# A decoder kernel: the order of projections and value products in a state-space layer, and of key products in the attention behind it

## The chip, the cores and the metric

The kernel runs on one core of a Trainium2 chip. It is one program for the whole two-layer decoder. The metric is the device time of one execution in microseconds (us); shown are the median and the extremes of three runs, and one further execution was taken by the hardware profiler. The engines are PE (TensorE, matmul), DVE (VectorE), ACT (ScalarE), POOL (GpSimd) and SP (SyncE, which here only issues DMAs). A product of one engine reaches another through SBUF or PSUM and a semaphore; each engine works its own list of instructions in order.

## The reference, cut to what matters

64 sequences of 128 tokens, width 128, go through two layers. The change touches two stages: the state-space layer L1_attn and the preparation of the values of the cross attention L1_xattn, and that cross attention.

```python
# state-space layer, E = 256 channels, N = 16 states
z = x @ W_in + b_in
xc, xr = z[..., :E], silu(z[..., E:])
xc = silu(conv(xc) + conv_b)                    # four taps
proj = xc @ x_proj_w                            # dt (16), B (16), C (16)
delta = softplus(dt @ dt_proj_w + dt_bias)      # the step size
h = exp(delta * A) * h + (delta * u) * B        # for each of 16 states, along time
y = sum_over_states(h * C) + u * D_param
out = (y * xr) @ W_out + b_out
# cross attention, 16 heads over a context of 77 tokens
q = x @ Wq + bq;  k = ctx @ Wk + bk;  v = ctx @ Wv + bv
out = softmax(q k^T / 8) v @ Wo + bo + x        # then layernorm
```

## The kernel before

**State-space layer** (`phase_scan`, L1522 on). The 64 sequences are worked in NG = 16 groups of four, so a tile is 128 partitions (channels) by 2 halves by 512 columns (4 x 128 tokens). Each group runs through 16 states, and each engine has a function `body(g, s)` with a loop `for n in range(states)`, into which all other work is hung by tests such as `if n == 5`. That hand-written place is what sets the order.

For a state n: ACT makes the decay factors, an exponential for each half (`decay_state`, L2030), into PSUM. POOL makes the drive (`drive_state`, L1877), three buffers deep. DVE scans both halves (`scan_state`, L2242) and, for the 13 inline states, multiplies by C (`read_state`, L2255); PE adds the result into `y_ps` by a product with the identity (`sum_state`, L2394). In the states 3, 7 and 13, called aside, POOL multiplies by C instead and PE adds three states later (`sum_aside`, L2402). ACT can write a half's decay only when DVE has scanned that half of the state before, as there is one PSUM buffer.

Between them stands work for the coming groups. PE: `turn` (transposes x of group g + 2), `project_bc` (dt, B and C for g + 1), `project_dt` (the step size product for g + 1), `project_conv` (two times four taps for g + 2), `project_res` (g + 2), and `project_out` for group g - 1. All use the two PSUM banks of `f_ps`. ACT copies these out: `copy_xT`, `copy_proj`, `take_raw` (the step size: an absolute value and a Relu), then `soft_exp` and `soft_ln` (with a table load before and one after), after which POOL's `make_delta` adds the two parts of the softplus. DVE gates y (`gate_y`) and adds the output to x (`leave_group`).

**Lots.** The same phase also multiplies the context by the attention's folded value and output weights and writes the result to DRAM: 39 lots of 128 context rows times 4 parts of 512 columns make 156 units. A unit is one matmul in a bank of `f_ps` (`make_lot`, L2322), one copy on ACT (`take_lot`, L2071) into one of three stage tiles, and one DMA on SP (`store_units`). The table `places` gives ten a group, each as (state in which PE makes it, bank, state in which ACT copies it; 16 and 17 are states 0 and 1 of the next group). So groups 0 to 14 have ten, group 15 has six.

SP's list in this phase holds, for each group, the loads of B and C rows (`load_b`, `load_c`), the store of these rows and the stores of the units, in a fixed order; a store waits for ACT's copy and whatever is behind it on SP waits too.

**Cross attention** (`phase_cross1`, L2518 on). It works one sequence a step, i from -7 to 65. In step i PE makes the scores of i + 2, turns the softmax of i (`turn_p`, three parts), multiplies it by the values (`mix`, the output), and makes the "front" work: four key products for seven elements ahead, until they run out, and one transpose of x for four ahead. The front products go in turn into the two banks of `f_ps` (`follow`: a product waits until the one two places before it has been copied by ACT). `plan[i]` splits the five into early, middle and late, and both PE and ACT take them in this order: PE early behind the second part of the turns, middle ahead of `mix`, late behind it; ACT early behind `copy_p(i, 1)`, middle ahead of the exponential of i + 2 (`exp`), late behind it. SP loads the values of element i + 2 (`load_values`); the first of these loads waits until all 156 units are in DRAM.

## Time and profile before

| | us |
|---|---|
| median of three runs | 2921.3 |
| lowest, highest | 2917.96, 2922.2 |
| profiled execution | 2918.92 |
| its span in the trace | 2917.0 |
| busy: PE, DVE | 2483.3, 2258.2 |
| busy: POOL, ACT | 2039.5, 1712.4 |

The span runs from the first to the last instruction in the trace; the device time of that same execution is 1.9 us longer. The scans of the state-space layer run from 1115 to 2073 us in the span, the scores of the attention from 2102 to 2637 us; these two stages are some half of the time. PE, DVE and POOL are all busy for most of the layer, so a share of busy time does not tell which one holds the others; the waits before single instructions in one group do.

### The profile page before, as it was taken

Reading aid. Unit: us, or ns where it says so; the run is one execution under the profiler, and the core shown is the slowest. Engines: PE = TensorE matmul, PEld = TensorE weight load, DVE = VectorE, ACT = ScalarE, POOL = GpSimd, SP = SyncE. Lnnn points to the kernel's source line nnn. Section 1 sums busy time; section 2 is a strip of 40 time slices with the busy share of each in tenths; the row PEclk is TensorE's granted clock in tenths of the full one; section 3 lists DMA queues with packets and bytes.
Section 4 is the critical chain, followed back from the end, with each engine's and each line's share of the span. In section 5 each row is a group of like instructions: output and inputs, shape, how many; then the busy total and the mean of one; then the engine's idle time right before and its main releaser. Section 6 shows DMA issues by size and latency. Waiting matters only on the chain. (4 is left out here: it accounts for less than half of the span.)

```text
span 2917.0 us, 43507 instructions
## 1 busy us (share of the span) xinstructions
PE 2483.3 (85%) x13043; PEld 1466.9 (50%) x13058; DVE 2258.2 (77%) x3693; ACT 1712.4 (59%) x3383; POOL 2039.5 (70%) x1817
## 2 busy tenths in 40 slices
PE   6969999899799957889999899897799999995555
PEld 4646666566556632333333333342367777773222
DVE  5979999666534469999899988999577777776887
ACT  7847777643222246767776676765355555554665
POOL 5539999567656638989999899998355555554454
PEclk9969999899899988999999999999999999997555
DMA  5911111011155535545545455555222222220000
GB/s 177 422 33 23 23 23 23 3 38 44 38 156 161 154 114 201 196 161 205 195 173 199 169 199 187 182 190 175 65 68 81 79 81 81 77 79 18 18 18 22
DMA packets 238424, 331.81 MB, mean 114 GB/s; under 512 B 46434, under 2 KB 186999, under 8 KB 217347
## 3 DMA queue, kind: packets, MB, share of 16 engines
q1 hardware_dynamic: 227538, 311.48, 32.5%
q0 software_dynamic: 9088, 16.94, 1.6%
q8 instruction: 105, 1.72, 0.2%
q14 instruction: 109, 0.89, 0.1%
q10 hardware_dynamic: 1584, 0.79, 0.1%
HBM read 231.45 MB, written 99.50 MB: 113 GB/s over the span
## 5 line engine op out<-in xcount | busy, mean ns | idle before, releaser
L1877 POOL TENSOR_TENSOR s_drive<-s_du,s_b_sb 128x1024 f32<-128x1024 f32 x256 | 599.8, 2359 | 30.9 <-DVE s_state_ps L2242 30.7
L2242 DVE TENSOR_TENSOR_SCAN s_state_ps<-s_decay_ps,s_drive 128x512 f32<-128x512 f32 x416 | 487.5, 1217 | 74.1 <-ACT s_decay_ps L2030 63.8
L2394 PE MATMUL s_y_ps<-s_read,w_ident 128*128 128x512 f32 x832 | 404.0, 612 | 73.9 <-DVE s_read L2255 73.4
L2030 ACT ACTIVATE s_decay_ps<-s_delta,neg_rate 128x508 f32<-128x508 f32 x512 | 342.4, 683 | 162.9 <-DVE s_state_ps L2242 151.5
L2394 PEld LDWEIGHTS s_y_ps<-s_read,w_ident 128*128 128x128 f32 x832 | 152.2, 192 | 306.7 <-issue 155.6
L2255 DVE TENSOR_TENSOR s_read<-s_state_ps,s_c_sb 128x1024 f32<-128x1024 f32 x208 | 254.6, 1224 | 7.2
L1421 POOL DMA_INDIRECT m_y_scratch<-e_y,e_index x156 | 152.5, 978 | 93.8 <-DVE e_y L1467 51.9
L2322 PE MATMUL s_f_ps<-w_c_wvo,s_lotT 128*128 128x512 f32 (+1 forms) x312 | 157.7, 603 | 45.5 <-ACT s_dtT L1998 20.8
L2684 POOL TENSOR_TENSOR c_share<-c_p,c_norm 128x1232 f32<-128x1232 f32 x64 | 147.5, 2305 | 65.3 <-DVE c_norm L2816 65.3
L2731 ACT ACTIVATE c_k<-c_f_ps,key_bias 128x308 f32<-128x308 f32 x256 | 132.4, 518 | 100.0 <-PE c_f_ps L2884 99.7
L742 ACT ACTIVATE b_pT<-b_turn_ps 77x512 f32<-77x512 f32 x256 | 144.3, 591 | 74.4 <-PE b_turn_ps L871 74.4
L2925 PE MATMUL c_turn_ps<-c_vp,c_pT 128*128 128x128 f32 (+1 forms) x1280 | 158.0, 279 | 21.3 <-ACT c_pT L2756 21.3
L2884 PE MATMUL c_f_ps<-c_ctxT,w_c_wqk 128*128 128x308 f32 x512 | 166.3, 430 | 7.1 <-DMA c_ctxT<-in_ctxT_dram 5.2
L2925 PEld LDWEIGHTS c_turn_ps<-c_vp,c_pT 128*128 128x128 f32 (+1 forms) x1280 | 147.7, 191 | 49.0 <-issue 49.0
L1045 POOL DMA_INDIRECT m_rows_scratch<-m_xs,m_index x128 | 128.2, 1002 | 60.4 <-issue 39.9
L676 POOL TENSOR_TENSOR b_p<-b_p,b_top 128x1232 f32<-128x1232 f32 x64 | 143.9, 2248 | 36.0 <-DVE b_top L803 36.0
L2797 DVE TENSOR_REDUCE c_top<-c_s_ps 128x16 f32<-128x1232 f32 x64 | 92.2, 1441 | 95.4 <-PE c_s_ps L2900 95.4
L2751 ACT ACTIVATE c_pT<-c_turn_ps 128x512 f32<-128x512 f32 x128 | 69.7, 595 | 150.4 <-PE c_turn_ps L2916 150.4
L2071 ACT ACTIVATE s_stage<-s_f_ps 128x512 f32<-128x512 f32 (+1 forms) x156 | 90.6, 590 | 106.1 <-PE s_f_ps L2322 104.7
L871 PE MATMUL b_turn_ps<-w_ident,b_p 128*77 128x128 f32 x1024 | 152.6, 282 | 0.0
L2900 PE MATMUL c_s_ps<-c_k,c_xT 128*128 128x308 f32 x512 | 148.5, 432 | 0.0
L2660 POOL TENSOR_TENSOR x<-c_xs,w_c_bo 128x128 f32<-128x128 f32 x64 | 31.2, 488 | 165.7 <-DVE c_xs L2792 165.7
(389 smaller groups left out, 6293.7 us busy)
## 6 DMA issues: line engine op xcount, KB each, us to landing
s_b_sb<-s_bc_scratch SPq DMA_DIRECT2D x64, 1024.0 KB, 5.8
s_c_sb<-s_bc_scratch SPq DMA_DIRECT2D x64, 1024.0 KB, 5.6
c_vp_scratch<-s_stage SPq DMA_DIRECT2D x152, 256.0 KB, 2.9
c_vp<-c_vp_scratch SPq DMA_DIRECT2D x64, 576.0 KB, 4.1
m_rows_scratch<-fill SPq DMA_DIRECT2D x33, 1040.0 KB, 27.1
e_w<-in_m_we_dram SPq DMA_DIRECT2D x39, 384.0 KB, 3.2
e_xg<-m_rows_scratch SPq DMA_DIRECT2D x39, 260.0 KB, 3.4
s_read<-m_y_scratch SPq DMA_DIRECT2D x32, 256.0 KB, 3.1
```

Of the source, the lines that this page charges most:

```text
L871: last = nc.tensor.transpose(turn_ps[0:S2, j % 2, r * 128:(r + 1) * 128], p[:, s, per * r + j, :], core.ident[:, :])
L1421: nc.gpsimd.indirect_dma_start(y_dram[:, :], bass.IndirectOffsetOnAxis(index[:, t % y_slots, j:j + 1], 0), y[:, t % y_slots, j, :], None, ...
L1877: nc.gpsimd.tensor_tensor(drive[:, (g * states + n) % drives, :, :], du[:, s, :, :], b_sb[:, n, :].unsqueeze(1).broadcast_to([128, halves, ...
L2030: nc.scalar.activation(decay[:, m, :, 1:], delta[:, s, m, :].rearrange("p (b t) -> p b t", t=T)[:, :, 1:], ACT.Exp, scale=core.neg_rate[:, ...
L2242: nc.vector.tensor_tensor_scan(home[:, h, :], decay[:, h, :, :].rearrange("p b t -> p (b t)"), drive[:, (g * states + n) % drives, h, :], ...
L2255: nc.vector.tensor_tensor(read[:, r % deep, :, :], state[:, :, :], c_sb[:, n // per_chunk % 2, n % per_chunk, :].unsqueeze(1).broadcast_to ...
L2322: nc.tensor.matmul(f_ps[0:lot_width(j), bank, :], lotT[:, j % lot_slots, 0:lot_width(j)], wvo[:, 4 * n:4 * n + 4, :].rearrange("p h d -> p ...
L2394: last = nc.tensor.matmul(y_ps[:, m, :], core.ident[:, :], read[:, r % deep, m, :], start=False, stop=False)
L2684: nc.gpsimd.tensor_tensor(share[:, i % 2, :].rearrange("p (s h) -> p h s", h=heads), p[:, i % p_slots, :, :], norm[:, i % 2, :].unsqueeze( ...
L2884: nc.tensor.matmul(f_ps[:, mine % 2, 0:GB * S2], core.w["c_wqk"][:, h, :], ctxT[:, g % 2, :], start=True, stop=True).then_inc(front_ready. ...
L2900: last = nc.tensor.matmul(scores[:, r, :, :], xT[:, i % xT_slots, :], k[:, g % 2, per * r:per * (r + 1), S2 * e:S2 * (e + 1)], start=True, ...
L2925: last = nc.tensor.matmul(y_ps, pT[0:width(c), i % 2, c, :], vp[0:width(c), i % vp_slots, c, :], start=(c == 0), stop=(c == lumps - 1))
```

## The change

It changes no arithmetic. In the layer's per-state lists:

- `project_dt` on PE goes from state 5 to 4, `take_raw` on ACT from 7 to 6, `soft_ln` from 9 to 10, POOL's `make_delta` from 11 to 12; `soft_exp` stays in 8. DVE's `leave_group` goes from state 4 to 3.
- The table of units becomes `slots_of(g)`: eight in each of groups 0 to 13, eighteen in group 14 (both banks in each of states 7 to 15), twenty-six in group 15 (bank 0 in states 0 to 13, bank 1 in 4 to 15). The places (3, 0, 5) and (7, 1, 9) are gone, and the second unit of state 6 is copied in state 9 instead of 8. 14 x 8 + 18 + 26 = 156.
- PE makes a state's units ahead of the projections of that state instead of behind them.
- SP's stores are placed by the state of the copy, and units left at the end are copied and stored behind the last group.

In the attention the order of the five front products becomes key, key, key, x, key, with the second and third in the middle part (before: the second alone). A load of values waits for the stores that its own element reads instead of all.

```diff
-        places = ((1, 0, 3), (3, 0, 5), (6, 0, 8), (6, 1, 8), (7, 1, 9), (10, 0, 12), (13, 0, 15), (13, 1, 15),
-                  (14, 1, 16), (15, 1, 17))
+        def slots_of(g):
+            if g < NG - 2:
+                return [(1, 0, 3), (6, 0, 8), (6, 1, 9), (10, 0, 12), (13, 0, 15), (13, 1, 15), (14, 1, 16), (15, 1, 17)]
+            if g == NG - 2:
+                return [(n, bank, n + 2) for n in range(7, states) for bank in range(2)]
+            return [(n, bank, n + 2) for n in range(states) for bank in range(2) if (n <= 13, n >= 4)[bank]]
...
-                    if n == 11 and ahead(g, 1):
+                    if n == 12 and ahead(g, 1):
                         make_delta(g + 1, 1 - s)
...
-                    if n == 7 and ahead(g, 1):
+                    if n == 6 and ahead(g, 1):
                         take_raw(g + 1, 1 - s)
                     if n == 8 and ahead(g, 1):
                         soft_exp(g + 1, 1 - s)
-                    if n == 9 and ahead(g, 1):
+                    if n == 10 and ahead(g, 1):
                         soft_ln(g + 1, 1 - s)
...
+            for unit in taken_at(NG, 0, states):
+                take_lot(unit)
...
-                    if n == 4 and behind(g, 1):
+                    if n == 3 and behind(g, 1):
                         leave_group(g - 1, 1 - s)
...
+                    for unit in made_at(g, n):
+                        make_lot(g, unit)
                     if n == 1 and behind(g, 1):
                         project_out(g - 1, 1 - s)
                     if n == 2 and ahead(g, 1):
                         project_bc(g + 1, 1 - s)
-                    if n == 5 and ahead(g, 1):
+                    if n == 4 and ahead(g, 1):
                         project_dt(g + 1, 1 - s)
...
-                    for unit in units_at("made", g, n):
-                        make_lot(g, unit)
...
             if on(i + ahead_turn):
-                here.append(("x", i + ahead_turn))
+                here.insert(len(here[:3]), ("x", i + ahead_turn))
...
-            plan[i] = (here[:1], here[1:2], here[2:])
+            plan[i] = (here[:1], here[1:3], here[3:])
...
-                if i == 0:
-                    for n, out in enumerate(lot_out):
-                        sp.wait_ge(out.sem, out.at(-(-(units - n) // len(lot_out)), 0))
+                stored = min(units, (((i + 1) * S2 - 1) // 128 + 1) * heads * 128 // 512)
+                for n, out in enumerate(lot_out):
+                    sp.wait_ge(out.sem, out.at(-(-(stored - n) // len(lot_out)), 0))
```

ACT in a middle group, from the decays of states 6 and 7 on, before. `s_decay_ps` are the decays (two a state), `s_stage` the copies of units, `s_conv_sig<-s_f_ps` and `s_delta` the two of `take_raw`, the other `s_conv_sig` the exponential and Ln of the softplus:

```order
L2030 ACTIVATE s_decay_ps<-s_delta,neg_rate 128x4x127 x4
L2008 ACTIVATE s_conv_sig<-s_f_ps 128x1024
L2009 ACTIVATE s_delta<-s_f_ps 128x1024
L2030 ACTIVATE s_decay_ps<-s_delta,neg_rate 128x4x127 x2
L2071 ACTIVATE s_stage<-s_f_ps 128x512 x2
L2013 ACTIVATE s_conv_sig<-s_conv_sig 128x1024
L2030 ACTIVATE s_decay_ps<-s_delta,neg_rate 128x4x127 x2
L2071 ACTIVATE s_stage<-s_f_ps 128x512
L2017 ACT_TABLE_LOAD
L2017 ACTIVATE s_conv_sig<-s_conv_sig 128x1024
L2030 ACT_TABLE_LOAD
L2030 ACTIVATE s_decay_ps<-s_delta,neg_rate 128x4x127 x4
```

And after, from `take_raw` on (line numbers being those of the changed kernel):

```order
L2006 ACTIVATE s_conv_sig<-s_f_ps 128x1024
L2007 ACTIVATE s_delta<-s_f_ps 128x1024
L2028 ACTIVATE s_decay_ps<-s_delta,neg_rate 128x4x127 x4
L2069 ACTIVATE s_stage<-s_f_ps 128x512
L2011 ACTIVATE s_conv_sig<-s_conv_sig 128x1024
L2028 ACTIVATE s_decay_ps<-s_delta,neg_rate 128x4x127 x2
L2069 ACTIVATE s_stage<-s_f_ps 128x512
L2028 ACTIVATE s_decay_ps<-s_delta,neg_rate 128x4x127 x2
L2015 ACT_TABLE_LOAD
L2015 ACTIVATE s_conv_sig<-s_conv_sig 128x1024
L2028 ACT_TABLE_LOAD
L2028 ACTIVATE s_decay_ps<-s_delta,neg_rate 128x4x127 x2
```

`take_raw` stands ahead of the decays of state 7 instead of behind them, one copy of a unit stands in state 8 instead of two, and Ln with its two table loads stands behind the decays of state 10.

PE in the same group, from the output product of the group before to the units of state 6, before. `s_f_ps<-w_c_wvo` are the units, `s_f_ps<-s_dtT` the step size product, `s_y_ps<-s_read` the sums (two matmuls a state):

```order
L2417 MATMUL s_f_ps<-w_s_w_out,s_res_gate 128x128 x8
L2322 MATMUL s_f_ps<-w_c_wvo,s_lotT 128x512
L2394 MATMUL s_y_ps<-s_read,w_ident 128x512 x2
L2363 MATMUL s_f_ps<-s_u,w_s_x_proj 48x512 x2
L2322 MATMUL s_f_ps<-w_c_wvo,s_lotT 128x512
L2394 MATMUL s_y_ps<-s_read,w_ident 128x512 x4
L2375 MATMUL s_f_ps<-s_dtT,w_s_dt_proj 128x512 x2
L2394 MATMUL s_y_ps<-s_read,w_ident 128x512 x2
L2402 MATMUL s_y_ps<-s_state_aside,w_ident 128x512 x2
L2322 MATMUL s_f_ps<-w_c_wvo,s_lotT 128x512 x3
```

And after, from the sums of states 0 and 1:

```order
L2390 MATMUL s_y_ps<-s_read,w_ident 128x512 x4
L2317 MATMUL s_f_ps<-w_c_wvo,s_lotT 128x512
L2413 MATMUL s_f_ps<-w_s_w_out,s_res_gate 128x128 x8
L2390 MATMUL s_y_ps<-s_read,w_ident 128x512 x2
L2358 MATMUL s_f_ps<-s_u,w_s_x_proj 48x512 x2
L2390 MATMUL s_y_ps<-s_read,w_ident 128x512 x2
L2371 MATMUL s_f_ps<-s_dtT,w_s_dt_proj 128x512 x2
L2390 MATMUL s_y_ps<-s_read,w_ident 128x512 x4
L2398 MATMUL s_y_ps<-s_state_aside,w_ident 128x512 x2
L2317 MATMUL s_f_ps<-w_c_wvo,s_lotT 128x512 x2
```

The unit of state 1 stands ahead of the output product, the one of state 3 is gone, and the step size product stands behind the sum of state 4 instead of 5.

PE in a middle step of the attention, from a step's scores (`c_s_ps`) to the next ones, before. `c_f_ps<-c_ctxT` are keys, `c_f_ps<-w_ident` the turn of x, `c_turn_ps<-c_vp` is mix:

```order
L2900 MATMUL c_s_ps<-c_k,c_xT 128x308 x4
L2916 MATMUL c_turn_ps<-w_ident,c_share 128x128 x8
L2884 MATMUL c_f_ps<-c_ctxT,w_c_wqk 128x308
L2916 MATMUL c_turn_ps<-w_ident,c_share 128x128
L2916 MATMUL c_turn_ps<-w_ident,c_share 80x128
L2884 MATMUL c_f_ps<-c_ctxT,w_c_wqk 128x308
L2925 MATMUL c_turn_ps<-c_vp,c_pT 128x128 x10
L2884 MATMUL c_f_ps<-c_ctxT,w_c_wqk 128x308 x2
L2876 MATMUL c_f_ps<-w_ident,c_xs 128x128
L2900 MATMUL c_s_ps<-c_k,c_xT 128x308 x4
```

And after, from the turns behind the scores:

```order
L2911 MATMUL c_turn_ps<-w_ident,c_share 128x128 x8
L2879 MATMUL c_f_ps<-c_ctxT,w_c_wqk 128x308
L2911 MATMUL c_turn_ps<-w_ident,c_share 128x128
L2911 MATMUL c_turn_ps<-w_ident,c_share 80x128
L2879 MATMUL c_f_ps<-c_ctxT,w_c_wqk 128x308 x2
L2920 MATMUL c_turn_ps<-c_vp,c_pT 128x128 x10
L2871 MATMUL c_f_ps<-w_ident,c_xs 128x128
L2879 MATMUL c_f_ps<-c_ctxT,w_c_wqk 128x308
L2895 MATMUL c_s_ps<-c_k,c_xT 128x308 x4
```

The third key has gone from behind mix to ahead of it, and the fourth from ahead of x to behind it.

## Rows read from the trace of the kernel before

**Rows 1.** The page: TensorE clock granted in each of the 40 equal slices of the span.

```profile
PEclk9969999899899988999999999999999999997555
```

**Rows 2.** Timeline of DVE, group 7: start us, us, what, [idle before <-releaser].

```profile
1557.82 2.35 DVE L2242 TENSOR_TENSOR_SCAN s_state_ps<-s_decay_ps,s_drive 128x512 f32<-128x512 f32 x2 [0.31 <-ACT s_decay_ps L2030]
...
1564.14 2.35 DVE L2242 TENSOR_TENSOR_SCAN s_state_ps<-s_decay_ps,s_drive 128x512 f32<-128x512 f32 x2 [0.47 <-ACT s_decay_ps L2030]
...
1569.19 2.35 DVE L2242 TENSOR_TENSOR_SCAN s_state_ps<-s_decay_ps,s_drive 128x512 f32<-128x512 f32 x2 [1.44 <-ACT s_decay_ps L2030]
...
1574.68 2.35 DVE L2242 TENSOR_TENSOR_SCAN s_state_ps<-s_decay_ps,s_drive 128x512 f32<-128x512 f32 x2 [1.88 <-ACT s_decay_ps L2030]
...
1578.37 2.34 DVE L2242 TENSOR_TENSOR_SCAN s_state_ps<-s_decay_ps,s_drive 128x512 f32<-128x512 f32 x2
...
1585.58 2.33 DVE L2242 TENSOR_TENSOR_SCAN s_state_aside<-s_decay_ps,s_drive 128x512 f32<-128x512 f32 x2
1588.03 2.35 DVE L2242 TENSOR_TENSOR_SCAN s_state_ps<-s_decay_ps,s_drive 128x512 f32<-128x512 f32 x2
```

**Rows 3.** Timeline of ACT, the same stretch.

```profile
1566.08 0.60 ACT L2071 ACTIVATE s_stage<-s_f_ps 128x512 f32<-128x512 f32 x1 [1.46 <-PE s_f_ps L2322]
1566.94 0.60 ACT L2071 ACTIVATE s_stage<-s_f_ps 128x512 f32<-128x512 f32 x1 [0.26 <-PE s_f_ps L2322]
1567.43 1.05 ACT L2013 ACTIVATE s_conv_sig<-s_conv_sig 128x1024 f32<-128x1024 f32 x1
...
1570.19 1.28 ACT L2017 ACT_TABLE_LOAD   x1
...
1573.86 1.29 ACT L2030 ACTIVATE s_decay_ps<-s_delta,neg_rate 128x508 f32<-128x508 f32 x2
...
1577.68 0.67 ACT L1957 ACTIVATE s_conv<-s_f_ps,s_conv_bias 128x512 f32<-128x512 f32 x1
...
1584.47 1.30 ACT L2030 ACTIVATE s_decay_ps<-s_delta,neg_rate 128x508 f32<-128x508 f32 x2
...
1587.23 1.40 ACT L2030 ACTIVATE s_decay_ps<-s_delta,neg_rate 128x508 f32<-128x508 f32 x2
```

**Rows 4.** Timeline of PE, the same stretch.

```profile
1559.48 1.98 PE L2375 MATMUL s_f_ps<-s_dtT,w_s_dt_proj 17*128 17x512 f32 x4
...
1568.61 1.88 PE L2394 MATMUL s_y_ps<-s_read,w_ident 128*128 128x512 f32 x4
1570.33 3.60 PE L2344 MATMUL s_f_ps<-s_xT,w_s_taps 128*128 128x512 f32 x8
```

**Rows 5.** Timeline of PE, one step of the attention.

```profile
2385.70 1.03 PE L2916 MATMUL c_turn_ps<-w_ident,c_share 128*128 128x128 f32 x8
2386.57 0.69 PE L2884 MATMUL c_f_ps<-c_ctxT,w_c_wqk 128*128 128x308 f32 x2
2387.09 0.38 PE L2916 MATMUL c_turn_ps<-w_ident,c_share 128*128 128x128 f32 x2
2387.31 0.68 PE L2884 MATMUL c_f_ps<-c_ctxT,w_c_wqk 128*128 128x308 f32 x2
2388.28 2.47 PE L2925 MATMUL c_turn_ps<-c_vp,c_pT 128*128 128x128 f32 x20 [0.29 <-ACT c_pT L2756]
2390.59 1.20 PE L2884 MATMUL c_f_ps<-c_ctxT,w_c_wqk 128*128 128x308 f32 x4
2391.97 0.30 PE L2876 MATMUL c_f_ps<-w_ident,c_xs 128*128 128x128 f32 x1 [0.18 <-ACT c_k L2731]
...
2394.25 1.03 PE L2916 MATMUL c_turn_ps<-w_ident,c_share 128*128 128x128 f32 x8
```

**Rows 6.** Timeline of ACT, the same step.

```profile
2387.30 0.52 ACT L2731 ACTIVATE c_k<-c_f_ps,key_bias 128x308 f32<-128x308 f32 x1
...
2388.85 1.23 ACT L2743 ACTIVATE c_p<-c_p 128x1232 f32<-128x1232 f32 x1 [0.30 <-DVE c_p L2804]
2391.31 1.03 ACT L2731 ACTIVATE c_k<-c_f_ps,key_bias 128x308 f32<-128x308 f32 x2 [1.23 <-PE c_f_ps L2884]
```

107 lines of the change are left out of this document (47 added, 60 removed).

## The prediction

> **What bounds the kernel now.** I first read the page's slices, then the timelines of DVE, ACT and PE side by side for one group of the state-space layer, then PE and ACT for one step of the cross attention. The layer's sixteen groups and the attention's 64 steps are the two places that the diff touches.
>
> In the state-space layer DVE sets the pace. From one inline state to the next it takes 3.69 us (1574.68 to 1578.37 [rows 2]), from an aside state to the next 2.45 us (1585.58 to 1588.03), and when nothing holds it a gap of 0.09 us (0.12 behind an aside state) is left between instructions. In four states it waits for ACT's decay factors: 0.31, 0.47, 1.44 and 1.88 us ahead of states 6, 8, 9 and 10 [rows 2]. Less the natural gaps that is 0.22 + 0.35 + 1.35 + 1.79 = 3.71 us a group. Rows 3 tell why. In state 8 ACT stands 1.46 us until PE has the first value product, then 0.26 us for the second, then does the exponential of the softplus (1567.43) and only then the decay. In state 9 another product copy and the two table loads around Ln stand before the decay: 1570.19 to 1573.86 = 3.67 us [rows 3].
>
> In the attention PE sets the pace: a step is 8.55 us (2385.70 to 2394.25 [rows 5]). PE works the whole step but for two holes. A key takes 0.52 us (the first, 2386.57, to the next turn, 2387.09). The second starts at 2387.31, so PE is free at 2387.83, yet mix starts at 2388.28: 0.45 us, in which the last copy of the turned probabilities is awaited. Mix occupies PE for 2390.59 - 2388.28 = 2.31 us. Behind the fourth key PE is free at 2390.59 + 1.04 = 2391.63, and the turn of x starts at 2391.97: 0.34 us, since x takes the PSUM bank of the third key, which ACT is still copying. Together 0.79 us a step.
>
> **Attention: third key ahead of mix.** No work is added. I put the start of the turns at 0. The third key wants the bank of the first, whose copy runs on ACT from 1.60 to 2.12 (2387.30 and its 0.52 us [rows 6]); the lag from such a copy's end to PE's start is 0.14 us by x: the first of the two copies from 2391.31 [rows 6] ends 0.52 us on, at 2391.83, and x starts at 2391.97 [rows 5]. So the third key runs from 2.26 to 2.78, most of it in what was the hole in front of mix (2.13 to 2.58). Mix starts at 2.78 instead of 2.58 and ends at 5.09. Then x (it shares its bank with the second key, copied long before), the fourth key, 0.52 us, and the scores. x and the scores take 2.28 us (2391.97 to 2394.25): the step ends at 7.89 us. Gain 8.55 - 7.89 = 0.66 us.
> What is late next: ACT's copy of the third key is now ahead of the next exponential. A key's copy follows the matmul's start by 0.73 us (2386.57 to 2387.30 [rows 5, 6]), so it runs from 2.99 to 3.51 and the exponential starts there instead of at 3.15 (2388.85), 0.36 us later. Behind that are DVE's sums and POOL's division, which serve a turn two steps later, over 8 us away: covered. If that cover were gone, the 0.36 us would come back and leave 0.30.
> Steps with keys and mix are 0 to 56, since keys run 7 elements ahead of 64: 57 steps. 57 x 0.66 = 38 us, which I take, since each part of it has its row. Bounds: 57 x 0.30 = 17 us, and 57 x 0.79 = 45 us if both holes close. The waits of the value loads on the stores of their own lots only, instead of all, cost nothing: three waits on SP, which is ahead by two elements, and the last lots are stored before the first keys are through.
>
> **Layer, the step size product at state 4.** The product ran on PE in state 5, from 1559.48 for 1.98 us [rows 4], so its copies on ACT could not start before 1561.5. Now it stands behind the sum of state 4, with no value product between them. The input that it waits for was already awaited, before, by the value product that went ahead of that same sum, so it is there. A read ends about when the next scan can start; without stalls scan 6 comes at 1557.6, so read 4 ends at 1557.6 - 3.69 = 1553.9, the sum takes 1.72 us (1568.61 to 1570.33), and the product is there near 1557.6, four us earlier. ACT copies it behind the decay of state 6, 1.0 us for each half of the work (1.05 us for 1024 columns, 1567.43 [rows 3]), and is ready for the decay of state 7 near 1559.6; the scan wants it by 1560.3. ACT's opening of the gate of the residual no longer follows a lot's copy (0.5 us), so the 0.22 us before state 6 go, and so do the 0.35 before state 8, where ACT has nothing to do in state 7. The leave of the group's output moves from behind a read to behind an aside scan; PE's output product is still issued two states ahead of it: no cost, 0.1 us at most.
>
> **State 8 to 9.** Time from the start of scan 6 (1557.82) from here on. The copy in state 8 still waits for a product that PE makes after the sum of state 6 and the aside sum of 3. Both follow the read of state 6, which follows scan 6. That chain does not move: copy at 8.26 (1566.08 [rows 3]). Now there is one copy, not two, so the exponential starts 0.49 us later (1566.94 to 1567.43) at 8.75 and the scan 1.76 us behind that (1567.43 to 1569.19) at 10.51. Scan 8 is at 6.32 - 0.35 = 5.97 (1564.14 less 1557.82 and the stall), so scan 9 would come at 9.66: 0.85 us stay of the 1.35. The second product's copy in state 9 fits in ACT's slack.
>
> **Ln in state 10.** ACT's work behind a decay starts 3.00 us behind the scan before (1574.68 to 1577.68 [rows 2, 3]); with 3.67 us for the block and 0.82 from the decay to the scan (1573.86 to 1574.68), scan 11 comes 7.49 us behind scan 9, free running 7.38: 0.11 us of 1.79 stay. POOL's softplus sum, moved from state 11 to 12, is wanted by the decays of the next group, four states on: no cost.
> The Trainium skill, ScalarE: Activation LUTs, section What ACT_TABLE_LOAD costs, puts a switch of tables at 1283 ns plus a drain of about 1380 ns. The trace has 1.28 us for the load and 3.67 us for both loads and Ln together [rows 3], so no such drain stands there and the row is used; by the page the block would be some 2.7 us longer (rival D).
>
> **What is late next: state 13.** PE's convolution of the group after next (1570.33) started a chain with no hole in it: convolution, sum, convolution, sums of state 10 and of aside 7, then the lot that ACT copies in state 12, one more copy, then the decay at 1584.47, 14.14 us later [rows 3, 4]. Before, the sum ahead of the convolution started at 1568.61 behind an extra product; now it starts when the read of state 8 ends, 3.69 us behind scan 8, at 9.66, and the convolution 1.72 us later at 11.38. The decay starts at 25.52, scan 13 at 26.34. Free running it is 10.51 + 3.69 + 3.80 + (1585.58 - 1578.37 = 7.21) = 25.21: a new stall of 1.13 us. Behind it come the four normalising instructions: decay to decay 1584.47 to 1587.23 = 2.76 us against 2.45 for the scans, 0.31 us more.
>
> **Sum for the layer.** Stalls before 3.71, after 0.85 + 0.11 + 1.13 + 0.31 = 2.40, gain 1.31 us a group, 14 groups (0 to 13): 18.3 us. Group 14 has no convolutions to run; its 18 lots, two a state, are 1.72 us of PE beside a 1.72 us sum in 3.69. There, two copies come before Ln in state 10, a stall of about 1.3 us, so 2.4 gained. Group 15 has 26 lots: I find 0.4 at the leave, 1.0 at state 9 and 0.8 at state 14, against 1.1 that go, and 0.4 us at the end, where the last lot's copy comes ahead of the last output product: 1.5 lost. These are estimates from the same durations. Layer: 18.3 + 2.4 - 1.5 = 19.2 us. Bounds: 14 x 3.71 = 52 us if no stall stays, and about -5 if the new chain on PE costs as much as the old stalls and the late lots of groups 14 and 15 cost three times what I find.
>
> **Total.** 38 + 19.2 = 57 us. The profiled execution took 2918.9 us, 1.9 around its span of 2917.0, and 2.4 under the median 2921.3. 2918.9 - 57 = 2862; from the median 2864. I give 2863.
>
> **Rivals.**
> A, the layer's stalls only move (PE's chain to state 13 takes all): attention alone, 2921 - 38 = 2883. For it: PE's chain from 1570.33 to 1584.47 has no hole. Against: the old stalls of states 6, 8 and 10 come to more than the chain holds back. 0.13.
> B, the attention gives half, because the later exponential hands its 0.36 us back: 17 + 19 = 36 us, 2885. Against it the two-step distance. 0.09.
> C, better: PE's idle records hide slack, the lot in state 12 is ready in time and most stalls go: 38 + 45 = 83 us, 2838. 0.10.
> D, the Ln block is longer in its new place by 2.7 us: scan 11 would come at 20.7, scan 13 at 27.9, the group would gain nothing, 2921 - 38 = 2883. It is one of the mechanisms at A's time; 0.02.
> E, slower: TensorE's clock. PE is busier in the attention (7.76 us of work in 7.89 instead of 8.55). The granted clock is in the top tenth there, and falls to 8 tenths in some earlier slices and to 5 at the end, where PE is idler [rows 1]. If fuller work lowered it, each step would be longer by its share: 57 x 7.89 = 450 us of PE; at 0.89 granted the 57 us are eaten (450 / 0.89 - 450 = 56), below it the change is slower; at 0.85, 2863 + 79 = 2942. Nothing in the rows shows a fall with fuller work. 0.03.
> F, no change: both gains lie under other waits of SP or DMA that appear when the steps are shorter. 0.03.
>
> **Numbers.** Forecast (2845 to 2877) 0.60; A, B, D together 0.24; C 0.10; E 0.03; F 0.03. To hold eight in ten the range takes the forecast and reaches to A, B and D: 2842 to 2886. A difference of 0.2%, 6 us, is what a measurement here can tell. Faster 0.94, same 0.03, slower 0.03.
>
> **What would show it.** The step of the attention reads 7.89 us, PE's hole ahead of mix is under 0.2 us and x follows mix at once. In a middle group DVE waits near 0.9 us ahead of state 9, 0.1 ahead of 11, 1.1 ahead of 13, none ahead of 6, 8 and 10, and the group takes 58.8 us instead of 60.2. I am wrong if the exponential's delay reaches DVE's next maximum, if state 13's stall is over 3 us, or if ACT stands for stores in group 15.

## The result and the profile after

The changed kernel takes 2855.7 us (median of 4 runs, 2851.9 to 2857.5); the kernel before, run beside it, 2920.6 us (4 runs, 2918.0 to 2922.2). The ratio is 0.9777, with a 95% interval of 0.9760 to 0.9794: 64.9 us, 2.2%, faster. The prediction said 2863 us, a gain of 57 to 58, in a range of 2842 to 2886: sign and range hold, and the gain is some 7 us larger than forecast.

The page of the changed kernel: span, busy time of each engine (share of the span, instructions), and the granted TensorE clock of the 40 slices.

```profile
span 2854.1 us, 43572 instructions
...
PE 2464.7 (86%) x13043; PEld 1470.7 (52%) x13058; DVE 2256.0 (79%) x3693; ACT 1706.6 (60%) x3383; POOL 2040.6 (71%) x1817
...
PEclk9969999999989988999999999999999999996555
```

The span is 2854.1 us against 2917.0. The clock line differs from that of [rows 1] in four of the 40 slices, by a tenth each. Over the attention's steps the granted clock reads 1.00 in both kernels (2110 to 2620 us before, 2110 to 2580 after): the attention did not lose clock for its fuller work, and rival E is out.

To place the difference I took two distances in each trace: from the first scan to the last (the layer) and from the first maximum of the attention to the last. The first pair of rows below has the scans and the maxima of the kernel before, the second pair those of the changed kernel (durations in ns, then the start of the first and of the last).

```profile
L2242 DVE TENSOR_TENSOR_SCAN s_state_ps<-s_decay_ps,s_drive x416: 1204/1206/1232, 1115.5 to 2070.8; 128x512 f32<-128x512 f32 x139
L2797 DVE TENSOR_REDUCE c_top<-c_s_ps x64: 1426/1441/1442, 2104.7 to 2635.2; 128x16 f32<-128x1232 f32 x64
```

```profile
L2242 DVE TENSOR_TENSOR_SCAN s_state_ps<-s_decay_ps,s_drive x416: 1204/1206/1232, 1115.3 to 2054.2; 128x512 f32<-128x512 f32 x139
L2792 DVE TENSOR_REDUCE c_top<-c_s_ps x64: 1378/1441/1442, 2088.3 to 2572.1; 128x16 f32<-128x1232 f32 x64
```

By these rows the layer went from 955.3 to 938.9 us; with the last double scan taken at the start of its first half, as below, from 954.2 to 937.7, 16.5 us shorter. The attention went from 530.5 to 483.8, 46.7 shorter. Together that is 63.2 us, and the spans differ by 62.9: what lies outside the two stretches adds up to 0.3 us.

**The layer, a middle group.** Timeline of DVE, changed kernel, group 7: the scans of states 6, 7 (aside), 8, 9, 11, 13 (aside) and 14; those of 10 and 12 start at 1560.86 and 1568.44, without a wait. Columns as in [rows 2], which this answers.

```profile
1546.66 2.35 DVE L2242 TENSOR_TENSOR_SCAN s_state_ps<-s_decay_ps,s_drive 128x512 f32<-128x512 f32 x2
...
1550.18 2.33 DVE L2242 TENSOR_TENSOR_SCAN s_state_aside<-s_decay_ps,s_drive 128x512 f32<-128x512 f32 x2
1552.42 2.32 DVE L2242 TENSOR_TENSOR_SCAN s_state_ps<-s_decay_ps,s_drive 128x512 f32<-128x512 f32 x2
...
1557.16 2.35 DVE L2242 TENSOR_TENSOR_SCAN s_state_ps<-s_decay_ps,s_drive 128x512 f32<-128x512 f32 x2 [1.16 <-ACT s_decay_ps L2028]
...
1564.74 2.35 DVE L2242 TENSOR_TENSOR_SCAN s_state_ps<-s_decay_ps,s_drive 128x512 f32<-128x512 f32 x2 [0.27 <-ACT s_decay_ps L2028]
...
1572.84 2.34 DVE L2242 TENSOR_TENSOR_SCAN s_state_aside<-s_decay_ps,s_drive 128x512 f32<-128x512 f32 x2 [0.80 <-ACT s_decay_ps L2028]
1575.58 2.35 DVE L2242 TENSOR_TENSOR_SCAN s_state_ps<-s_decay_ps,s_drive 128x512 f32<-128x512 f32 x2 [0.41 <-ACT s_decay_ps L2028]
```

The waits of states 6, 8 and 10 are gone. A wait stays ahead of 9, and new ones stand ahead of 11, 13 and 14. ACT and PE of the same stretch say why; ACT first, then PE.

```profile
1554.91 0.60 ACT L2069 ACTIVATE s_stage<-s_f_ps 128x512 f32<-128x512 f32 x1 [1.68 <-PE s_f_ps L2317]
1555.41 1.05 ACT L2011 ACTIVATE s_conv_sig<-s_conv_sig 128x1024 f32<-128x1024 f32 x1
1556.35 1.29 ACT L2028 ACTIVATE s_decay_ps<-s_delta,neg_rate 128x508 f32<-128x508 f32 x2
...
1560.25 1.28 ACT L2015 ACT_TABLE_LOAD   x1
...
1563.92 1.29 ACT L2028 ACTIVATE s_decay_ps<-s_delta,neg_rate 128x508 f32<-128x508 f32 x2
...
1570.95 0.60 ACT L2069 ACTIVATE s_stage<-s_f_ps 128x512 f32<-128x512 f32 x1 [3.15 <-PE s_f_ps L2317]
...
1572.02 1.30 ACT L2028 ACTIVATE s_decay_ps<-s_delta,neg_rate 128x508 f32<-128x508 f32 x2
```

```profile
1544.78 1.98 PE L2371 MATMUL s_f_ps<-s_dtT,w_s_dt_proj 17*128 17x512 f32 x4
...
1557.88 3.60 PE L2339 MATMUL s_f_ps<-s_xT,w_s_taps 128*128 128x512 f32 x8
```

State 9 waits because ACT stood 1.68 us for the value product, then made the exponential, then the decay. State 13 waits because ACT stood 3.15 us for the next value product, which on PE is the last in a row without a hole behind the convolution. The step size product runs at 1544.78, 1.88 us before scan 6; in [rows 2, 4] it ran 1.66 us behind it.

**The attention, one step.** Timeline of PE, changed kernel; it answers [rows 5].

```profile
2240.57 1.03 PE L2911 MATMUL c_turn_ps<-w_ident,c_share 128*128 128x128 f32 x8
2241.44 0.68 PE L2879 MATMUL c_f_ps<-c_ctxT,w_c_wqk 128*128 128x308 f32 x2
2241.97 0.38 PE L2911 MATMUL c_turn_ps<-w_ident,c_share 128*128 128x128 f32 x2
2242.18 1.42 PE L2879 MATMUL c_f_ps<-c_ctxT,w_c_wqk 128*128 128x308 f32 x4
2243.44 2.39 PE L2920 MATMUL c_turn_ps<-c_vp,c_pT 128*128 128x128 f32 x20
2245.67 0.27 PE L2871 MATMUL c_f_ps<-w_ident,c_xs 128*128 128x128 f32 x1
2245.78 0.68 PE L2879 MATMUL c_f_ps<-c_ctxT,w_c_wqk 128*128 128x308 f32 x2
2246.30 2.24 PE L2895 MATMUL c_s_ps<-c_k,c_xT 128*128 128x308 f32 x8
2248.38 1.03 PE L2911 MATMUL c_turn_ps<-w_ident,c_share 128*128 128x128 f32 x8
```

The second and third key are one row of four matmuls (2242.18), mix follows at 2243.44 and x at once behind it. The step is 2248.38 - 2240.57 = 7.81 us against 8.55. ACT of the same step, answering [rows 6]: the copy of the third key and the exponential behind it.

```profile
2243.64 0.52 ACT L2726 ACTIVATE c_k<-c_f_ps,key_bias 128x308 f32<-128x308 f32 x1 [0.22 <-PE c_f_ps L2879]
2244.05 1.22 ACT L2738 ACTIVATE c_p<-c_p 128x1232 f32<-128x1232 f32 x1
```

**The last two groups.** Measured from scan to scan, groups 0 to 13 are together 21.6 us shorter (a middle one 58.69 us instead of 60.19), but group 14 is 2.0 longer (59.96 to 61.95) and group 15 with its 15 distances 3.1 longer (53.40 to 56.50). In group 14, first PE:

```profile
1953.15 3.56 PE L2390 MATMUL s_y_ps<-s_read,w_ident 128*128 128x512 f32 x4 [2.51 <-DVE s_read L2255]
1956.64 1.98 PE L2371 MATMUL s_f_ps<-s_dtT,w_s_dt_proj 17*128 17x512 f32 x4
```

PE has no value product to do here, stands 2.51 us, and the sum that follows takes 3.56 us where the same four matmuls take 1.88 to 1.98 elsewhere: the granted clock of this stretch reads 0.54, so nearly all of it ran at the lower of the two levels, 1.2 and not 2.4 GHz. The step size product comes late by that, and scan 7 follows scan 6 by 4.42 us instead of 3.52. Later in the group, ACT and then SP, the DMA issues (their time is that of the issuing):

```profile
1984.45 0.60 ACT L2069 ACTIVATE s_stage<-s_f_ps 128x512 f32<-128x512 f32 x1 [1.15 <-DMA c_vp_scratch<-s_stage]
...
1991.53 0.60 ACT L2069 ACTIVATE s_stage<-s_f_ps 128x512 f32<-128x512 f32 x1 [4.66 <-DMA c_vp_scratch<-s_stage]
```

```profile
1981.61 0.50 SPq L1746 DMA_DIRECT2D s_c_sb<-s_bc_scratch  x1
1983.33 9.13 SPq L1772 DMA_DIRECT2D c_vp_scratch<-s_stage  x4
```

ACT stands for a staging tile whose store has not landed, 4.66 us. Stores of a unit take 2.4 us at the median from issue to landing, 8.1 us at most. Behind that wait scan 15 comes 7.07 us after scan 14 instead of 3.69. PE has no work meanwhile; its next unit and the sum behind it, and then DVE's gate of y at the start of group 15:

```profile
1992.22 2.05 PE L2317 MATMUL s_f_ps<-w_c_wvo,s_lotT 128*128 128x512 f32 x2 [4.17 <-issue]
1994.06 3.50 PE L2390 MATMUL s_y_ps<-s_read,w_ident 128*128 128x512 f32 x4
```

```profile
2002.81 1.22 DVE L2264 TENSOR_TENSOR s_res_gate<-s_y_ps,s_res_gate 128x1024 f32<-128x1024 f32 x1 [2.67 <-PE s_y_ps L2398]
```

Behind its 4.17 us without work PE is slow again: 2.05 us for the unit instead of 1.10 and 3.50 for the sum instead of 1.88, at a granted clock of 0.51 from 1992.2 to 1997.4 us. From there to the last aside sum its list has no hole, and DVE, which waits 0.15 us for that sum in other groups, waits 2.67: scan 1 of group 15 follows scan 0 by 7.42 us instead of 4.90. So the late store is paid twice, once through ACT and once through PE.

### The profile page after: what moved, and what is told of

It is laid out like the page before. It is cut to its first block and busy times, and to the rows that moved or that the text cites. A ratio compares the mean times of both kernels' runs of the same rounds, so it can differ in the third digit from the quotient of the medians.

```text
span 2854.1 us, 43572 instructions
## 1 busy us (share of the span) xinstructions
PE 2464.7 (86%) x13043; PEld 1470.7 (52%) x13058; DVE 2256.0 (79%) x3693; ACT 1706.6 (60%) x3383; POOL 2040.6 (71%) x1817
## 3 DMA queue, kind: packets, MB, share of 16 engines
q8 instruction: 105, 1.72, 0.3%
## 5 line engine op out<-in xcount | busy, mean ns | idle before, releaser
L2879 PE MATMUL c_f_ps<-c_ctxT,w_c_wqk 128*128 128x308 f32 x512 | 178.5, 437 | 8.6 <-DMA c_ctxT<-in_ctxT_dram 5.0
L2808 DVE TENSOR_REDUCE c_norm<-c_p 128x16 f32<-128x1232 f32 x64 | 91.9, 1436 | 69.9 <-ACT c_p L2738 69.9
L682 POOL TENSOR_TENSOR b_p<-b_p,b_norm 128x1232 f32<-128x1232 f32 x64 | 144.0, 2250 | 2.3 <-DVE b_norm L809 2.2
```

Of the source, the lines that this page charges most:

```text
L2879: nc.tensor.matmul(f_ps[:, mine % 2, 0:GB * S2], core.w["c_wqk"][:, h, :], ctxT[:, g % 2, :], start=True, stop=True).then_inc(front_ready. ...
```

## The experiments

Each kernel ran beside the kernel before, whose median was 2919.5, 2919.9 and 2920.4 us in the three sets. "Layer" is the distance from first to last scan, "attention" that from first to last maximum; in the changed kernel 937.7 and 483.8 us, before 954.2 and 530.5 (for a double scan the start of its first half is taken). wait_all, x_last, third_late and after_again are one execution each, and rest on their traces.

**Each part alone.** att_only is the kernel before with the new plan of the attention:

```
-                here.append(("x", i + ahead_turn))
+                here.insert(len(here[:3]), ("x", i + ahead_turn))
...
-            plan[i] = (here[:1], here[1:2], here[2:])
+            plan[i] = (here[:1], here[1:3], here[3:])
```

> The kernel before with the attention's new order of the five front products alone; the layer, its units and the wait of the values' loads are as before. Theory (the gain is two separate sums): the attention loses the 46.7 us that the trace of the changed kernel shows between the first and the last maximum (530.5 to 483.8 us), the layer keeps 954.2 us from its first to its last scan, and the time is 2921 - 47 = 2874 us. Rival (the shorter layer helps the attention, or the loads of values do): the attention gains less than 42 us alone.

Measured: 2874.9 us, ratio 0.9841 (0.9825 to 0.9858), a gain of 44.7; layer 955.1, attention 485.4, a step 7.80. The attention gives 45.1 of the 46.7 us; the missing 1.7 are in one place, the scores of the third step, which take 4.00 us here and 2.31 in the changed kernel, at a granted clock of 0.56 against 1.00, behind a wait of 0.73 us in both.

layer_only is the changed kernel with these two lines turned back.

> The changed kernel with the attention's front products in the old order. Theory: the layer takes 937.7 us, the attention 530.5 us, time 2921 - 17 = 2904 us. Rival (the units that are stored late in the layer delay the attention): a first maximum of scores later than 35.3 us behind the last scan, time over 2908 us.

Measured: 2901.8 us, ratio 0.9937 (0.9921 to 0.9954), a gain of 17.8; layer 932.3, attention 530.5. 44.7 + 17.8 = 62.5 against 64.9 for both: the parts add up within the spread of the runs, and neither hides under the other. In the traced execution the layer is 5.4 us shorter than in the changed kernel's, with the same instructions in it; it was also the fastest of its four (2897.9 to 2905.2 us). More on that below.

**The attention's gain: the third key, not x.** x_last is the changed kernel with x behind the fourth key again, the third key still ahead of mix:

```
-                here.insert(len(here[:3]), ("x", i + ahead_turn))
+                here.append(("x", i + ahead_turn))
```

> The changed kernel with x put back behind the fourth key; the third key stays ahead of the output product. Theory: it is the third key's place alone that counts, since x then wants the bank of the third key, which has been copied during the output product: step 7.8 us, as with x ahead. Rival (moving x closed the hole of 0.34 us ahead of x): step 8.1 to 8.2 us, 57 x 0.34 = 19 us slower than the changed kernel.

Measured: 2851.7 us, step 7.80, attention 485.3. The place of x is worth nothing in a full step. The first three distances are 1.7 us longer than in the changed kernel (6.58, 7.07, 7.80), but that is again the scores of the third step alone, 3.99 us at a granted clock of 0.57, as in att_only, where x does stand ahead. So that x's place is worth anything there is not shown.

third_late takes the other half back, the key behind mix, with x still ahead of the fourth key:

```
-            plan[i] = (here[:1], here[1:3], here[3:])
+            plan[i] = (here[:1], here[1:2], here[2:])
```

> The changed kernel with the third key back behind the output product, x still ahead of the fourth key. Theory (a bank of the two is free only when ACT has copied the key in it, 1.25 us behind the key's start, and PE starts 0.14 us on): the hole of 0.45 us ahead of the output product is back, and the fourth key, which now follows the third after 0.66 us, waits 0.7 us: a step of 8.9 us, 57 x 1.1 = 63 us slower than the changed kernel. Rival (the two holes are worth their 0.45 and 0.34 us singly): a step of 8.2 us.

Measured: 2932.3 us, slower than before; a step 8.94. Its PE timeline:

```profile
2382.55 2.47 PE L2920 MATMUL c_turn_ps<-c_vp,c_pT 128*128 128x128 f32 x20 [0.29 <-ACT c_pT L2751]
...
2385.38 0.27 PE L2871 MATMUL c_f_ps<-w_ident,c_xs 128*128 128x128 f32 x1
2386.24 0.76 PE L2879 MATMUL c_f_ps<-c_ctxT,w_c_wqk 128*128 128x308 f32 x2 [0.59 <-ACT c_k L2726]
```

The hole ahead of mix is back (0.29, as in [rows 5]), and the hole behind it is larger: the fourth key wants the bank of the third, whose matmul started only 1.38 us before, and waits 0.59 us for its copy. So both holes of [rows 5] are one cause, the third key's place: ahead of mix it fills the first, and its copy is over long before the fourth key asks for the bank. The kernel is 77 us slower than the changed one where 63 were expected. The 56 full steps give 64 of them; 7.7 more are in the first three steps, which the expectation left out, and 5.2 lie ahead of the first scan (1120.5 instead of 1115.3 us), where both kernels have the same instructions, and so are not shown to be the edit's.

**The waits of the value loads.** wait_all has the value loads wait once for all stores, as before:

```
-                stored = min(units, (((i + 1) * S2 - 1) // 128 + 1) * heads * 128 // 512)
-                for n, out in enumerate(lot_out):
-                    sp.wait_ge(out.sem, out.at(-(-(stored - n) // len(lot_out)), 0))
+                if i == 0:
+                    for n, out in enumerate(lot_out):
+                        sp.wait_ge(out.sem, out.at(-(-(units - n) // len(lot_out)), 0))
```

> The changed kernel with the loads of values waiting for all 156 units again. Theory: no difference (under 1 us), since the last unit is stored at 2062 us of the span and the first load of values is issued at 2083 us. Rival: the first load and the first output come later, and the first three steps (6.58, 5.84 and 7.36 us) grow back towards 8.9, 7.2 and 8.6.

Measured: 2851.5 us, attention 483.7, the first steps 6.58, 5.84, 7.36 us as in the changed kernel. The finer wait buys nothing.

**Ln in its old place.** ln_back:

```
-                    if n == 12 and ahead(g, 1):
+                    if n == 11 and ahead(g, 1):
                         make_delta(g + 1, 1 - s)
...
-                    if n == 10 and ahead(g, 1):
+                    if n == 9 and ahead(g, 1):
                         soft_ln(g + 1, 1 - s)
```

> The changed kernel with Ln and its two table loads back in state 9 and POOL's softplus sum back in state 11. Theory (PE's chain from the first convolution to the unit of state 12 sets when scan 13 comes, and stalls ahead of it are hidden in it): scan 10 comes 1.8 us later (a cadence of 5.5 instead of 3.7), but scan 13 only 0.7 us later, and the group takes 59.0 to 59.4 us instead of 58.7: 4 to 10 us slower. Rival (the stalls add): the whole 1.8 us stay, 60.3 us a group, 22 us slower.

Measured: 2855.8 us, ratio 0.9777 (0.9762 to 0.9792), where 4 to 10 us more than the changed kernel were expected: the two can't be told apart. In the traces a middle group takes 58.88 us, 0.19 more, and groups 0 to 13 together 3.3 us more. Its DVE timeline, scans of states 9, 10 and 13 (11 and 12 have no wait):

```profile
1560.45 2.35 DVE L2242 TENSOR_TENSOR_SCAN s_state_ps<-s_decay_ps,s_drive 128x512 f32<-128x512 f32 x2 [1.16 <-ACT s_decay_ps L2028]
...
1565.95 2.35 DVE L2242 TENSOR_TENSOR_SCAN s_state_ps<-s_decay_ps,s_drive 128x512 f32<-128x512 f32 x2 [1.89 <-ACT s_decay_ps L2028]
...
1576.85 2.33 DVE L2242 TENSOR_TENSOR_SCAN s_state_aside<-s_decay_ps,s_drive 128x512 f32<-128x512 f32 x2
```

The old 1.89 us ahead of state 10 is back in full, 1.80 in the distance of the scans, and costs 0.19: the distances into 11, 13 and 14 are 0.19, 0.88 and 0.49 us shorter and have no wait left (3.69, 3.52 and 2.25). Counted from scan 9, scan 13 comes 0.72 us later, as expected; that 14's wait would go too was missed. What stood in state 10 had only moved to 13 and 14. So Ln's new place, which the largest single wait of [rows 2] suggests, is worth next to nothing by itself.

**The chain on PE.** If the chain is what holds state 9 and state 13, the value product must come earlier in it. lots_first puts it ahead of the aside sum in states 6 and 10 of groups 0 to 13, and changes nothing else:

```
+                    if n - 3 in aside and n < states - 1 and g < NG - 2:
+                        for unit in made_at(g, n):
+                            make_lot(g, unit)
                     if n == states - 1:
                         sum_aside(g, aside[-1])
                     elif n - 3 in aside:
                         sum_aside(g, n - 3)
-                    for unit in made_at(g, n):
-                        make_lot(g, unit)
+                    if not (n - 3 in aside and n < states - 1 and g < NG - 2):
+                        for unit in made_at(g, n):
+                            make_lot(g, unit)
```

> The changed kernel, but in states 6 and 10 of groups 0 to 13 PE makes the units ahead of the aside sum instead of behind it; the same instructions. Theory (ACT's copies in states 8 and 12 wait for PE's chain, in which the aside sum of 1.72 us stands): the copy in state 8 comes 1.7 us earlier and the stall ahead of state 9 (4.74 instead of 3.69) goes, the one ahead of state 13 (4.41 instead of 3.52) goes or is under 0.3, the one ahead of 14 stays; the group takes 56.8 to 57.2 us, 14 x 1.7 = 24 us less. Rival (ACT or POOL is the true bound): under 8 us less.

Measured: 2832.3 us, ratio 0.9703 (0.9688 to 0.9717); a middle group 56.97 us instead of 58.69, 14 x 1.72 = 24 us, and the layer is 24.5 shorter. Its DVE timeline, scans of states 9, 13 and 14, and ACT's copy of the unit that answers 1554.91 above:

```profile
1544.21 2.35 DVE L2242 TENSOR_TENSOR_SCAN s_state_ps<-s_decay_ps,s_drive 128x512 f32<-128x512 f32 x2
...
1559.24 2.34 DVE L2242 TENSOR_TENSOR_SCAN s_state_aside<-s_decay_ps,s_drive 128x512 f32<-128x512 f32 x2 [0.16 <-ACT s_decay_ps L2028]
1561.98 2.35 DVE L2242 TENSOR_TENSOR_SCAN s_state_ps<-s_decay_ps,s_drive 128x512 f32<-128x512 f32 x2 [0.40 <-POOL s_drive L1875]
```

```profile
1541.31 0.60 ACT L2069 ACTIVATE s_stage<-s_f_ps 128x512 f32<-128x512 f32 x1
```

ACT no longer stands for the product, the wait ahead of 9 is gone (3.67 us from scan 8 to scan 9 instead of 4.74) and most of that ahead of 13 (3.77 instead of 4.40; 3.52 without a wait). What is late next is POOL, with 0.40 us ahead of state 14. The chain is shown as the cause: the same work, with two neighbours in the other order, takes away one wait and most of the other, and the time follows.

**The store that lands late in group 14.** load_later moves two 1 MB loads of group 15's inputs behind the stores of the units, in group 14 alone:

```
-                if g + 1 < NG:
+                if g + 1 < NG and g != NG - 2:
                     load_c(g + 1, 0)
                 store_lots(g, 13, 16)
+                if g == NG - 2:
+                    load_c(g + 1, 0)
```

(and load_b of part 3 likewise, behind load_c of part 1).

> The changed kernel, but in group 14 SP issues the loads of the first C rows and the last B rows for group 15 behind the stores of the units instead of ahead of them. Theory (the units' stores queue behind two 1 MB loads, 8.1 us to landing, and ACT stands 4.66 us for one of the three stage tiles): the cadence of 7.07 us in state 14 of group 14 goes to under 4.5, the one of 7.42 in state 0 of group 15 to about 5, 5 to 7 us less. Rival (three stage tiles are too few for two units a state, wherever the loads stand): the wait only moves to the next state, under 2 us less.

Measured: 2852.2 us, ratio 0.9764 (0.9749 to 0.9779). Group 14 falls to 58.36 us and scan 15 is on time, 3.67 us; but group 15 takes 58.24 us, since DVE now stands for the load that was moved:

```profile
2001.24 1.23 DVE L2259 TENSOR_TENSOR s_read<-s_state_ps,s_c_sb 128x1024 f32<-128x1024 f32 x1 [3.18 <-DMA s_c_sb<-s_bc_scratch]
```

The longest wait of ACT for a store is now 1.35 us. In the trace the last two groups take 116.6 us together, 1.9 less than in the changed kernel's trace, where 5 to 7 were expected; the median is 3.5 us lower, which the intervals do not separate. The wait for the stores has moved to the reader of the load. That this is due to the order of loads and stores alone is not shown, since the same two groups also take 113 us with the order unchanged, as the last experiment tells. lots_first_load_later has this and lots_first together.

> Both edits together: units ahead of the aside sums in states 6 and 10, and the two loads of group 14 later. If both theories hold the gains add: about 24 + 6 = 30 us under the changed kernel, near 2826 us. If only one holds, 2832 to 2850 us.

Measured: 2831.5 us, ratio 0.9693 (0.9680 to 0.9706), some 5 us above what both gains together would give: the loads' place adds nothing that could be told from lots_first. In the traces the last two groups are 1.8 us shorter than in lots_first (115.8 against 117.7), and group 0, with the same instructions in both, is 2.6 us longer.

tail_early keeps lots_first, and makes one unit of group 14 in state 1 instead of state 12, in order to give PE work ahead of the step size product and take one store from the crowded end:

```
-                return [(n, bank, n + 2) for n in range(7, states) for bank in range(2)]
+                return [(1, 0, 3)] + [(n, bank, n + 2) for n in range(7, states) for bank in range(2)
+                                      if (n, bank) != (12, 1)]
...
-                if 5 <= n < 8 and ahead(g, 1) or g == NG - 2:
+                if 5 <= n < 8 and ahead(g, 1) or g == NG - 2 and n >= 5:
```

> The kernel with units ahead of the aside sums (groups 0 to 13), and in group 14 one unit moved from state 12 to state 1, so that PE has work there. Theory (in group 14 PE stands idle 2.5 us ahead of the sum of state 4, its clock falls, that sum takes 3.56 instead of 1.88 us and the step size product comes late): the cadence of 4.4 us in state 6 of group 14 goes back to 3.52, and the wait for a stage tile in state 14 gets shorter, 1 to 4 us less in all, near 2829 us. Rival (the product is late for another reason): 4.4 us stays.

Measured: 2830.2 us, ratio 0.9693 (0.9679 to 0.9707); group 14 takes 57.97 us, group 15 53.98. PE at the place of 1953.15 above:

```profile
1932.22 1.98 PE L2391 MATMUL s_y_ps<-s_read,w_ident 128*128 128x512 f32 x4 [1.84 <-DVE s_read L2256]
1934.14 1.98 PE L2372 MATMUL s_f_ps<-s_dtT,w_s_dt_proj 17*128 17x512 f32 x4
```

The sum runs at full speed (granted clock 1.00), and scan 7 follows scan 6 by 3.52 us. In all ten traces with the eighteen units of group 14 in states 7 to 15, PE stands 2.51 us at this place and the distance is 4.4 to 4.5: this 0.9 us is shown. ACT's long waits for a store are gone as well, but they are short too in three executions without this edit (below), so that is not shown to be its doing. By its median this is the fastest kernel of the study; its interval overlaps those of lots_first and lots_first_load_later, so it can't be told from them.

**Is the late store chance?** after_again is the changed kernel, unaltered, in another set.

> The changed kernel as it is, once more. Theory (how long ACT stands for a stage tile in group 14 depends on how its stores fall among the 1 MB loads of that execution): groups 0 to 13 as before to 0.02 us, groups 14 and 15 together between 112.9 and 118.5 us. Rival (the long wait belongs to the program): 7.07 and 7.42 us again.

Measured: 2854.5 us; groups 14 and 15 together 118.1 us, after 118.45 in the first. third_late, with the same instructions in the layer, has 118.3; but wait_all, x_last and layer_only, again with the same ones, have 112.95, 113.2 and 113.1. So the same layer takes one of two times that lie some 5 us apart. Three traced executions each way don't tell whether the program decides it or the execution: that the changed kernel had the longer one twice speaks for the program, the four runs of layer_only, which spread over 7 us with the traced one the fastest, for the execution.

What differs between the two times can be read. In the three longer ones PE stands 4.17, 2.77 and 2.08 us ahead of a unit in state 14 or 15 of group 14, and behind it the granted clock is 0.50 to 0.51; in the three shorter ones it stands 1.0 us there and goes on at full clock, and DVE's gate waits 0.15 us instead of 2.7 to 3.1. That makes group 15 some 2.5 to 3.0 us longer (56.50 to 56.95 us against 53.98), about what the slow rows lose: 0.95 us in the unit and, from start to start, 1.63 in the sum. The other 2.2 to 3.0 us are in group 14, where the stores land later. No run holds PE's clock up at this place, so its share is argued from the rows; why the stores land later in one execution than in another stays open. More than three staging tiles were not tried.

Group 0 shows the same thing without any store. In load_later, lots_first_load_later and tail_early it takes 59.6, 57.7 and 57.7 us, where the kernels that have the same instructions in this group take 56.8 (after) and 55.1 (lots_first). PE of load_later, the step size product behind a sum that waited 1.91 us:

```profile
1134.70 3.77 PE L2375 MATMUL s_f_ps<-s_dtT,w_s_dt_proj 17*128 17x512 f32 x4
```

The same product takes 1.98 us in the changed kernel, where the sum waited the same 1.91 us. The granted clock from 1132.2 to 1144 us is 0.57 in the three, 1.00 in the changed kernel and in lots_first. These 2.6 to 2.8 us are taken out of what the traces of the three gain at the other end, and differences of this size between single executions should not be read as the work of an edit.

## Why the prediction was right, point by point

**Bound by DVE in the layer, by PE in the attention: right.** The two parts add up (44.7 + 17.8).

**Third key ahead of mix, 0.66 us a step: right in mechanism, 0.08 us too small.** The third key was put at 2.26 us and mix at 2.78; mix starts at 2243.44 - 2240.57 = 2.87. But it occupies PE for 2245.67 - 2243.44 = 2.23 us where 2.31 was taken from [rows 5], and x and the fourth key begin 0.11 and 0.52 us apart with scores of 2.08 us instead of 2.14. Work that stands without a wait behind other work costs 0.06 to 0.08 us less than the rows of before, where it stood behind a hole. So 56 steps gave 0.745 us each, 41.8 us. The exponential moved by 0.33 us (2244.05 is 3.48 into the step, against 3.15), forecast 0.36, and its cover held: rival B is out.

**The start of the attention: not in the sum.** Its first three distances are 4.9 us shorter in total (8.91, 7.21, 8.57 to 6.58, 5.84, 7.36). Before, x waited 2.27 and 2.21 us for ACT's copy of the third key, which stood behind an exponential; PE of the kernel before shows it:

```profile
2109.39 0.30 PE L2876 MATMUL c_f_ps<-w_ident,c_xs 128*128 128x128 f32 x1 [2.27 <-ACT c_k L2731]
2109.60 3.93 PE L2900 MATMUL c_s_ps<-c_k,c_xT 128*128 128x308 f32 x8
```

In x_last, where x also comes last but the third key stands in the middle part, these waits are 0.18 us: here too it is the third key's place. Some 1.6 us of the 4.9 are the clock: the scores behind the first of these waits take 3.93 us, at a granted clock of 0.57, instead of 2.30. I costed the full steps alone and left the first ones at nothing; they were in the trace and could have been read.

**Step size product at state 4: right.** The product is through 0.1 us behind the start of scan 6 (1544.78 + 1.98 against 1546.66), as said, and the waits of states 6 and 8 are gone. The leave of the output costs nothing: the two distances around it are 2.42 + 4.16 before, 2.83 + 3.75 after, 6.58 both times.

**State 9: scan 9 comes 10.51 us behind scan 6 (1557.16 less 1546.66 is 10.50), forecast 10.51.** The wait itself reads 1.07 beyond the natural gap, not 0.85: scan 8, behind the aside scan, comes at 5.76 instead of the 5.97 that I took from [rows 2]. The 2.45 us that I read as an aside distance without a wait held one: without a wait it is 2.24 us, at this place after the change and in group 14 of the kernel before. So the old stalls were 0.55 us ahead of state 8, not 0.35, and 0.21 ahead of state 14, which I had at nothing.

**State 11: 0.18 us, forecast 0.11. The Ln block is 1560.25 to 1563.92, 3.67 us again:** rival D is out, and the row of before carried over. The Trainium skill, ScalarE: Activation LUTs, section What ACT_TABLE_LOAD costs, would put two drains of about 1380 ns there beside the loads; this trace has none: 1.28 + 1.06 + 1.28 us for load, Ln and load leave 0.05 of the 3.67.

**State 13: right, and 0.25 us too large.** Scan 13 follows scan 12 by 4.40 us, and by 3.52 without a wait: a stall of 0.88, forecast 1.13. (The row reads 0.80, but an aside scan that does not wait starts 0.08 us ahead of the end of the read before it.) The convolution starts at 11.22 us (forecast 11.38), the decay at 25.36 (25.52) and scan 13 at 26.18 (26.34): the chain between is 14.14 us to the digit, and begins 0.16 earlier since PE's sum of state 8 does. The other 0.09 is that scan 11 comes 7.58 us behind scan 9, not 7.49, so that 13 is wanted later. ln_back shows that the mechanism is this chain and not Ln, and lots_first removes most of it.

**State 14: 0.29 more than before, forecast 0.31.** Against a distance without a wait its stall is 0.50 now and was 0.21.

**The sum for a group.** From scan to scan, after less before: -0.21 us ahead of state 6, -0.55 ahead of 8, -0.31 ahead of 9, -1.79 ahead of 10, +0.19 ahead of 11, +0.88 ahead of 13, +0.29 ahead of 14. That is -1.50; forecast were -0.22, -0.35, -0.50, -1.79, +0.11, +1.13 and +0.31, together -1.31. Groups 0 to 13 give 21.6 us (forecast 18.3). Rival A is out.

**Groups 14 and 15: this term was wrong.** I put them at 2.4 gained and 1.5 lost; they lost 2.0 and 3.1, 6.0 us worse. The step that failed is the sentence that the eighteen value products of group 14 fit beside the sums, with no cost but Ln's 1.3 us (scan 11 of that group comes at 5.11, so that one held). Two things are missing in it: PE stands idle 2.51 us ahead of the sum of state 4 and then runs at half clock just when the step size product is queued behind that sum (0.9 us), and two units a state mean two stores a state into a queue that also carries 1 MB loads. These stores land late, ACT waits for a staging tile, PE runs dry and falls to half clock a second time (some 5 us in this execution, none of it in three others with the same layer). In those three the two groups together are 0.2 to 0.4 us shorter than before, against the 0.9 of the forecast. Of the signs of being wrong that the prediction names, ACT's waiting for stores in group 15 came true, 1.60 and 1.38 us, and cost nothing: the scans of those states are 3.69 to 3.70 us apart, as without a wait.

So the total was near for a partly wrong reason: 57 forecast, + 9 in the attention, + 3 in groups 0 to 13, - 6 in the last two, makes 63.

## What to carry to other kernels

Where a matmul waits for the bank of a copy that is still running, put between them the work that needs neither; one matmul moved closed two holes here. When the step that sets the pace has several waits in a row, removing an upstream one pays only until the chain of another engine decides: name that chain and reorder inside it, which gave 24 us here, more than the change itself gave in the layer. The first and last repetitions of a loop are to be costed from their own rows, since what they lack (work that keeps PE going, room in a DMA queue) is what makes them differ.

## What the runs showed of the hardware

A gap on PE can cost more than its length: behind 2.51 us of idling a sum of four matmuls took 3.56 us instead of 1.88 to 1.98 (granted clock 0.54), and in the kernel before, behind 2.27 us, the scores took 3.93 instead of 2.30 (0.57). Behind 1.84 us in tail_early, and behind another 2.21 us in the kernel before, they took their usual time. The length of the last gap alone does not decide it: behind the same 1.91 us in group 0 the clock fell in three traces and held in the changed kernel and lots_first, and behind the same 0.73 us the scores of the attention's third step took 4.00 us in att_only and 2.31 in the changed kernel. A page of slices does not show this, for the granted clock of the whole layer reads 0.99.

A store of 256 KB from the same issuing engine as 1 MB loads lands after 2.4 us at the median and 8.1 at most. Who waits for it is ACT, then PE for ACT, and PE's clock falls in that wait. The same instructions in the layer give either 118 or 113 us for two groups, and what decides it stays open.
